# Second attention of a two-layer kernel: output projection in four pieces, the copy of the maxima later, denominators moved by single transfers

## The reference, cut to what matters

```
x = x + L0_attn(layernorm(x))      # differential attention, 16 heads of 64
x = x + L0_ffn(layernorm(x))       # shared expert and top-1 of 8 experts
x = x + L1_attn(layernorm(x))      # the stage that is changed
x = x + L1_ffn(layernorm(x))       # x is 2 x 1024 x 128

def L1_attn(x):                    # B = 2, T = 1024, C = 128, H = 16, Dh = 8
    q, k, v = x @ wq.T + bq, x @ wk.T + bk, x @ wv.T + bv     # 16 heads of 8
    scores = einsum('bthd,bshd->bhts', q, k) * Dh ** -0.5     # masked keys: -inf
    attn = softmax(scores)
    return einsum('bhts,bshd->bthd', attn, v) @ wo.T + bo
```

## Time and profile before

| | us |
|---|---|
| three runs | 1717.89, 1722.80, 1723.13 (median 1722.8) |
| profiled execution, its own time | 1719.14 |
| its span | 1717.3 |
| busy in the span: PE, DVE, ACT, POOL | 1566.3, 1344.3, 1273.0, 963.6 |
| unit 0's first step to unit 6's second half | 1341.3 to 1620.4 |
| mean granted clock of TensorE | 0.959 |

### The profile page before, as it was taken

How to read it: one execution, slowest core, us unless ns; L and a number is a source line. 1 busy time by engine, 2 the same in 40 slices (tenths; PEclk the granted TensorE clock), 3 DMA queues, 4 the chain that set the end, 5 groups by cost and what they waited for, 6 DMA issues and landing times.

```text
span 1717.3 us, 28177 instructions
## 1 busy us (share of the span) xinstructions
PE 1566.3 (91%) x10531; PEld 653.9 (38%) x10531; DVE 1344.3 (78%) x2075; ACT 1273.0 (74%) x2052; POOL 963.6 (56%) x661
## 2 busy tenths in 40 slices
PE   5899999999999999999999999985776899999985
PEld 2444444444444444444444444433551222222223
DVE  6687877788777877787777877767778999999946
ACT  4777888888888888888888888873242688888872
POOL 2799877878788877888787887880000000111112
PEclk9999999999999999999999999997686899999998
DMA  4011011101011111101110101000000000000001
GB/s 125 22 27 23 21 29 33 25 23 27 22 37 23 23 25 37 26 21 26 27 35 22 27 23 33 22 11 3 1 22 23 2 16 16 17 17 14 15 14 32
DMA packets 50435, 42.37 MB, mean 25 GB/s; under 512 B 26021, under 2 KB 39242, under 8 KB 50298
## 3 DMA queue, kind: packets, MB, share of 16 engines
q1 hardware_dynamic: 50298, 40.55, 10.0%
HBM read 20.27 MB, written 1.31 MB: 13 GB/s over the span
## 4 chain that ended last, share of the span: by engine, by line
PE 74%; DVE 10%; issue 9%; ACT 5%; POOL 1%; DMA 1%; SPq 1%; ACTq 0%; POOLq 0%; DVEq 0%
PE PS L1439 20%; PE PS L1451 16%; PE PS L1463 13%; PE PS L1789 4%; PE PS L1506 4%; PE PS L1487 3%; PE PS L1756 2%; DVE mxp L1345 2%; PE PS L1773 2%; PE PS L1477 2%; PE PS L1523 2%; PE PS L1729 1%; DVE region L1041 1%; ACT region L766 1%; ACT ering L935 1%
## 5 line engine op out<-in xcount | busy, mean ns | idle before, releaser
L1027 DVE TENSOR_REDUCE nmx<-PS 128x1 f32<-128x1024 f32 x512 | 622.1, 1220 | 193.3 <-PE PS L1440 193.0
L567 POOL TENSOR_TENSOR ering<-ering 128x1024 f32<-128x1024 f32 x256 | 603.4, 2357 | 21.4
L748 ACT ACTIVATE ering<-PS,nmx 128x1024 f32<-128x1024 f32 x512 | 570.3, 1114 | 42.3 <-DVE nmx L1027 41.9
L565 POOL TENSOR_SCALAR ering<-ering,rho 128x1024 f32<-128x1024 f32 x256 | 286.3, 1119 | 220.9 <-DVE rho L1036 217.9
L1439 PE MATMUL PS<-region 64*128 64x512 f16 x1536 | 404.4, 380 | 6.1 <-DMA region<-region 4.2
L1440 PE MATMUL PS<-region 64*128 64x512 f16 x1536 | 404.4, 380 | 0.0
L1451 PE MATMUL PS<-ident,ering 128*128 128x128 f32 x2048 | 334.9, 286 | 8.8 <-ACT t L759 6.4
L1345 DVE TENSOR_REDUCE mxp<-PS 128x2 f32<-128x1024 f32 x256 | 303.8, 1221 | 30.1 <-PE PS L1773 26.5
L935 ACT ACTIVATE ering<-PS 128x1024 f32<-128x1024 f32 x256 | 260.3, 1024 | 76.4 <-PE PS L1756 68.6
L1451 PEld LDWEIGHTS PS<-ident,ering 128*128 128x128 f32 x2048 | 215.5, 141 | 259.4 <-issue 222.1
L1439 PEld LDWEIGHTS PS<-region 64*128 64x128 f16 x1536 | 112.3, 94 | 248.8 <-ACT ering L748 72.2
(11 more groups left out here) (286 smaller groups left out, 1855.1 us busy)
## 6 DMA issues: line engine op xcount, KB each, us to landing
region<-region SPq DMA_DIRECT2D x64, 256.0 KB, 3.7
osb<-scr SPq DMA_DIRECT2D x32, 128.0 KB, 3.2
rcp<-scr SPq DMA_DIRECT2D x32, 128.0 KB, 3.3
rcp<-scr SPq DMA_DIRECT2D x64, 64.0 KB, 2.0
x<-in_L_attn_X SPq DMA_DIRECT2D x4, 256.0 KB, 3.1
wq_raw<-in_L_attn_Wq SPq DMA_DIRECT2D x16, 64.0 KB, 3.2
wk_s<-in_L_attn_Wk SPq DMA_DIRECT2D x16, 64.0 KB, 1.8
wo_s<-in_L_attn_Wo SPq DMA_DIRECT2D x32, 32.0 KB, 2.6
```

What stands on the lines that cost most here:

```text
L565: P.tensor_scalar(e2, e2, rho[:, s:s + 1], 1.0, ALU.mult, ALU.mult).then_inc(s_scl_ok, 1)
L567: P.tensor_tensor(e1, e1, e2, ALU.subtract).then_inc(s_sub_ok, 1)
L748: A.activation((E1, E2)[p][s % 4], PS[:, bank:bank + 2, :].rearrange("p a b -> p (a b)"), ACT.Exp, bias=nmx[:, 2 * s + p:2 * s + p + 1], s ...
L1027: V.tensor_reduce(nmx[:, 2 * s + p:2 * s + p + 1], PS[:, bank:bank + 2, :].rearrange("p a b -> p (a b)"), AX.X, ALU.max, negate=True).then ...
```

## The change

- `to_out1` works in four parts of 128 columns instead of two of 256: at t = 13 to 16 for a unit's second half of before, and at t = 29, 30, 31 and step 0 of the next unit for its first half. In the loop after the last unit all four stand at t = 14.
- `copy_y1` moves with the last part: from t = 15 to 16, and from t = 31 to step 0 of the next unit.
- `ct_copy1` moves from t = 3 and 19 to t = 5 and 21.
- The four DMAs of `sums_out1` become one with a source of four rows; the four of the way back become one with the source `[4, 32, 512]`, whose middle dimension is a broadcast.
- SP's order changes: the write of the inverses to DRAM (`inverses_out1`) now stands directly behind the sums, ahead of `c_rows1`; only the last transfer (`inverses_back1`) stays behind `c_rows1`.
- `invert1` moves from t = 7 and 23 to t = 5 and 21, `turn_z1(0)` from t = 2 to t = 4.

```diff
@@ sync: second attention
-                for j in range(4):
-                    sp.dma_start(rc[32 * j:32 * j + 32, 0, :],
-                                 osb[32 * j + 8:32 * j + 9, :].rearrange("o (p c) -> o p c", c=16)).then_inc(s_sum_dma1, 16)
-
-            def sums_back1(hf):
-
+                sp.dma_start(rc[:, 0, :], osb[8:128:32, :].rearrange("j (p c) -> j p c", c=16)).then_inc(s_sum_dma1, 16)
+
+            def inverses_out1(hf):
                 sp.wait_ge(s_rc1_ok, hf + 1)
                 sp.dma_start(scr1.rearrange("(p c) -> p c", c=16), rc[:, 1, :]).then_inc(s_scr_dma1, 16)
+
+            def inverses_back1(hf):
+
                 sp.wait_ge(s_scr_dma1, 16 * (hf + 1))
                 if hf > 0:
                     sp.wait_ge(s_on1_ok, hf)
-                for j in range(4):
-                    sp.dma_start(rcp[32 * j:32 * j + 32, :], scr1[j * HF:j * HF + HF].rearrange(
-                        "(o q) -> o q", o=1).to_broadcast([32, HF])).then_inc(s_rcp_dma1, 16)
+                sp.dma_start(rcp[:, :], scr1.rearrange("(j o q) -> j o q", j=4, o=1).to_broadcast(
+                    [4, 32, HF])).then_inc(s_rcp_dma1, 16)
...
                 if n >= 1:
                     sums_out1(2 * n - 1)
+                    inverses_out1(2 * n - 1)
                 if 0 <= n < last1:
                     c_rows1(n, 1)
                 if n >= 1:
-                    sums_back1(2 * n - 1)
+                    inverses_back1(2 * n - 1)
...
@@ scalar
-                    if t == 3 and 0 <= n < last1:
+                    if t == 5 and 0 <= n < last1:
                         ct_copy1(2 * n + 1)
-                    if t == 19 and n + 1 < last1:
+                    if t == 21 and n + 1 < last1:
                         ct_copy1(2 * (n + 1))
...
-                    if t == 15 and n >= 1:
+                    if t == 0 and n >= 1:
+                        copy_y1(2 * n - 2)
+                    if t == 16 and n >= 1:
                         copy_y1(2 * n - 1)
-                    if t == 31 and 0 <= n < last1:
-                        copy_y1(2 * n)
@@ vector
-                    if t == 7 and n >= 1:
+                    if t == 5 and n >= 1:
                         invert1(2 * n - 1)
-                    if t == 23 and 0 <= n < last1:
+                    if t == 21 and 0 <= n < last1:
                         invert1(2 * n)
@@ tensor
-                at = slice(256 * part, 256 * part + 256)
+                at = slice(128 * part, 128 * part + 128)
                 mm = MM(MISC[:, at], wo1[:, hf // 4, :], on[:, at], start=True, stop=True)
-                if part == 1:
+                if part == 3:
                     mm.then_inc(s_y1_mm, 1)
...
-                    if t in (14, 15) and n >= 1:
-                        if own:
-                            pe.wait_ge(s_ct_ev1, 2 * n + 2)
-                        to_out1(2 * n - 1, t - 14)
+                    if t == 0 and n >= 1:
+                        to_out1(2 * n - 2, 3)
+                    if t == 13 and own and n >= 1:
+                        pe.wait_ge(s_ct_ev1, 2 * n + 2)
+                    if 13 <= t < 17 and own and n >= 1:
+                        to_out1(2 * n - 1, t - 13)
+                    if t == 14 and n == last1:
+                        for part in range(4):
+                            to_out1(2 * n - 1, part)
...
-                        if t == 2:
+                        if t == 4:
                             turn_z1(0)
...
-                    if t in (30, 31) and own:
-                        if nxt:
-                            pe.wait_ge(s_ct_ev1, 2 * (n + 1) + 1)
-                        to_out1(2 * n, t - 30)
+                    if t == 29 and own and nxt:
+                        pe.wait_ge(s_ct_ev1, 2 * (n + 1) + 1)
+                    if t >= 29 and own:
+                        to_out1(2 * n, t - 29)
```

More of the change, by code:

```diff
@@ L526, in _ @@
                 if n >= 1:
-                    sums_back1(2 * n - 1)
+                    inverses_back1(2 * n - 1)
                 if 0 <= n < last1:
                     sums_out1(2 * n)
+                    inverses_out1(2 * n)
                 if n + 1 < last1:
@@ L532, in _ @@
                 if 0 <= n < last1:
-                    sums_back1(2 * n)
+                    inverses_back1(2 * n)
             ov = out.rearrange("b (k p) e -> p (b k) e", p=128)
@@ L661, in weigh1 @@
             def weigh1(hf):
-                pool.wait_ge(s_rcp_dma1, 64 * (hf + 1))
+                pool.wait_ge(s_rcp_dma1, 16 * (hf + 1))
                 if hf > 0:
@@ L1287, in invert1 @@
             def invert1(hf):
-                dve.wait_ge(s_sum_dma1, 64 * (hf + 1))
+                dve.wait_ge(s_sum_dma1, 16 * (hf + 1))
                 if hf > 0:
```

## The result

The changed kernel takes 1743.3 us (median of 4 runs, 1742.6 to 1746.2) against 1721.9 of the kernel before on the same chip. The ratio is 1.0133, 95% interval 1.0118 to 1.0149: slower by 1.3%, 15 us above the forecast of 1728 and outside its range.

What follows compares the result with a forecast made beforehand. DVE was taken to set the pace of most steps and PE of some, both near their limit. Terms +0.8 + 2.2 + 5.2 - 3.3 = +4.9 on the 1722.8 us median gave 1728 us, range 1713 to 1740.

Steps and rivals of the forecast that it cites:

- Part 3: Sums' and inverses' single transfers: sums cost nothing; inverses land after 4.3 us, PE stalls 0.4 us 13 times, +5.2 us.
- 128 KB more than the 3.3 at that pace is 1.0, so I take 4.3: Inverses' 256 KB transfer: landing of 4.3 us, from 3.3 for 128 KB plus 1.0 at 131 GB/s.
- Rival (a): Inverses' transfer runs on four DMA engines: 4.8 us, stall 0.9, +6.5 us more; 1735 us, chance 0.24.
- the bound of 3.7: Lower bound in us for the landing of the inverses' single 256 KB transfer; with it the stalls cost 0.
- Part 5: Unit 7 and behind: earlier sums remove nearly all of PE's 2.97 us stall; together -3.3 us (-5 to -1).
- The two late pieces: Unit 7: first projection pieces of halves 13 and 14, expected to be late by 0.6 and about 2.0 us.
- Part 2: Product's copy one step later delays POOL; PE waits 0.6 us, 0.27 reaches DVE in eight halves: +2.2 us.
- Part 1: Projection in four pieces of 0.38 us, DVE losing 0.28 at each: +0.06 us a half, +0.8 us over 13.
- Part 4: Maxima's copy on ACT two steps later: ACT has about 3.6 us free in each half, so it costs nothing.
- Sums: Up to unit 6 the sums' single transfer lands before the earlier inversion, with 1.1 us of cover: cost nothing.
- (d): Sums' single transfer lands after 3 us, stalling DVE a few tenths each half; 5 us more, 1733; chance 0.04.

Runs made afterwards that it cites:

- sums_one: Kernel before with one edit: the four transfers of the sums became one; ratio 0.9955 to the kernel before.
- two_parts: Changed kernel with inverses back in four transfers and projection, product's copy and `turn_z1` as before the change; ratio 0.9968 to the kernel before.
- pool_order: Changed kernel with inverses back in four transfers and POOL's add of the earlier product behind both halves of `parts1`; ratio 0.9993 to the kernel before.
- four_back: Changed kernel with only the way back of the inverses in four transfers of 32 partitions again; ratio 1.0031 to the kernel before.
- run 8: Changed kernel with both inverses and sums in four transfers again, the inversion staying two steps earlier; ratio 1.0058 to the kernel before.
- run 9: The same run as `sums_one`: kernel before with only the sums' four transfers made one; ratio 0.9955 to the kernel before.
- four_narrow: Changed kernel with inverses back in four transfers, each with source `[4, 8, 512]` in place of `[32, 512]`; 1761.5 us, one run.
- two_back: Changed kernel with inverses back in two transfers of 64 partitions, each with source `[2, 32, 512]`; 1816.6 us, one run.

## Why the prediction was wrong

Laid end to end, the runs are a ladder from before to after (halves 0 to 12, then unit 7, us):

| step | halves 0-12 | unit 7 |
|---|---|---|
| sums by one transfer (`sums_one` less before) | +0.0 | -3.8 |
| inversion, maxima's copy and SP's order moved (`two_parts` less `sums_one`) | +0.9 | +0.1 |
| four pieces, POOL reordered (`pool_order` less `two_parts`) | -0.1 | +2.8 |
| POOL's add in front of `parts1` (`four_back` less `pool_order`) | +3.2 | +3.8 |
| inverses by one transfer (after less `four_back`) | +12.9 | +2.9 |
| sum | +16.9 | +5.7 |

**Part 3, the step that failed.** "128 KB more than the 3.3 at that pace is 1.0, so I take 4.3": the pace of 131 GB/s is that of transfers on many engines, and the new transfer runs on four. POOL started 4.7 to 5.2 behind its issue, PE stalled 0.84 to 1.40, 1.15 on average, and not 0.4, and twelve halves paid 12.9 us where 5.2 had been put for thirteen stalls. The start 0.7 us earlier (forecast 0.8) and the place of the stall were right. Rival (a) had the mechanism, the landing (4.8) and nearly the stall (0.9), and was given 0.24. The rows couldn't decide it, but the bound of 3.7 for "as `region<-region` of this size" came from a row of other tiles, and the middle between ends far apart hid that one end was a different mechanism.

**Part 5, the sign of the end.** Forecast -3.3, measured +5.7 in unit 7 and nothing behind it. The gain was there: `sums_one` shows -3.8, and PE's wait of 2.97 us at `turn_x4(0)` is gone in the kernel after. The other parts came on top of it: the ladder has +2.8 for the pieces, +3.8 for POOL's add in front of `parts1` and +2.9 for the inverses' transfer. Unit 7 of the kernel after, with the waits of PE for POOL that are longer than in the halves before:

```profile
1661.48 0.59 ACT L917 ACTIVATE yc<-PS 128x512 f32<-128x512 f32 x1
1662.15 1.26 POOL L685 TENSOR_TENSOR yT<-yT,yc 128x512 f32<-128x512 f32 x1 [6.92 <-ACT yc L917]
...
1664.10 0.42 PE L1797 MATMUL PS<-ident,c 128*8 128x128 f16 x4 [1.80 <-POOL c L677]
...
1679.41 0.46 PE L1803 MATMUL PS<-on,wo 128*128 128x128 f32 x2 [1.76 <-POOL on L666]
...
1687.92 0.66 PE L1820 MATMUL PS<-ident,yT 128*128 128x128 f32 x4 [1.17 <-POOL yT L685]
...
1701.82 0.78 PE L1803 MATMUL PS<-on,wo 128*128 128x128 f32 x2 [2.32 <-POOL on L666]
```

PE waits 1.80 us here for the split maxima behind POOL's add, where it waited 0.67 in the steady halves. The two late pieces had been listed, at 0.6 and 2.0, and their waits came out at 1.76 and 2.32. Not listed were the 1.80 and the wait for POOL's sum in front of `turn_z1(0)`, 1.17 us where it was 0.3 before. The clock dips after all, in other places: it is 0.78 from 1664.10 to 1672.00 and 0.72 from 1701.80 to 1708.00, behind the 1.80 and the 2.32, where `sums_one` and `two_parts` have 1.00 over all of unit 7. What each wait and the clock cost by itself wasn't separated. Rival (a)'s 1735 fell 8 us short mostly for this reason: it had -2.3 at the end.

**Part 2** had the right place (from the fifth half on, the turned maxima behind POOL) and the wait (0.67 against 0.6), but more of it reached DVE: 0.40 us a half, +3.2 against +2.2. **Part 1**: a piece costs 0.42 and not 0.38, DVE idles 0.30 in its steps (0.28 forecast), and the twelve halves came out at -0.1 together, not +0.8: DVE's idle time in front of the maxima is 24.2 us in `two_parts` and 24.0 in `pool_order`, so with it in four places other waits of DVE shrink. Bounded well, and small. **Part 4** cost no more than +0.9, together with the moves of the inversion and of SP's order; which of them makes it wasn't tried. Sums: right, no inversion waited up to half 12, so (d) didn't come, and run 8 shows that with four transfers they would have waited.

What was not tried: a single transfer of the inverses whose first dimension is 32 on both sides, which would tell the number of issues from the number of engines once more.

## What to carry to other kernels

Before joining transfers, look at the first dimension of both sides: the joined transfer can run on fewer engines, and then its time grows with its bytes per engine. That harmed a 256 KB transfer that is waited for and was harmless for one of 8 KB, where the saved issues were all that counted. Cost each part of a change once more at the stage's end, where the slack that hides it in the steady part is missing. And when a change has parts of both signs, run the part that is thought free by itself: here it was the one worth having.

## What the runs showed of the hardware

- A busy DMA engine moved 20 to 24 KB/us where two or four engines worked (99 GB/s by 0.26 of sixteen is 24, 46 by 0.13 is 22, 78 by 0.24 is 20), and 15 in `four_back` (122 by 0.51). The kernel before had 21.5 with transfers of the same shape as `four_back`.
- A broadcast dimension counts as the first one: `[4, 8, 512]` with both leading steps at zero ran on a quarter of the engines, though it reads the same 2 KB over and over.
- SP issued a transfer with a source of `[4, 8, 512]` in 0.64 us (2.56 for four), one of `[32, 512]` in 0.44 (1.75 for four).
- The four sums of 2 KB in one transfer landed 1.9 us behind their issue, though on a source of four rows (run 9, 1641.65 to 1643.54).
- With longer waits of PE the granted clock was lower: 1.00 with waits of up to 1.4 us a half, 0.96 with up to 1.9, 0.91 with up to 4.2 (halves 0 to 12 of the kernel after, `four_narrow`, `two_back`).
